# Layer 0's z rows and gates in two DRAM tensors, each gathered on its own

## The reference, cut to what matters

```
probs = softmax(z @ Wr + br)              # 8 experts
gate  = probs * keep                      # the most likely experts up to a mass of 0.8
h = relu(einsum('bth,ehf->betf', z, W1) + b1)      # F = 1024
y = einsum('betf,efh->beth', h, W2) + b2
out = einsum('bte,beth->bth', gate, y)
```

## Time and profile before

| | before |
|---|---|
| median of 3 runs | 1335.82 us (1334.29 to 1337.52) |
| the profiled execution: its own time | 1337.58 us |
| its span in the profile | 1335.9 us, so 1.7 us lie around the span |
| PE busy / DVE / ACT / POOL | 85% / 74% / 49% / 37% |
| layer 0's block loop | from about 188 us to about 650 us of the span |
| gathers of layer 0 on POOL | 76, mean 2.77 us |
| gathers of layers 1 and 2 on POOL (rows of 1,024 bytes) | 44, mean 1.19 us |

### The profile page before, as it was taken

One profiled execution on the slowest core, in us unless ns is written; L12 is line 12 of the kernel. 1 busy time (PEld: TensorE's weight loads), 2 busy tenths in 40 slices (PEclk: granted clock), 3 DMA queues, 4 the chain that ended last, 5 costly groups with the idle time before them and its releaser, 6 DMA issues.

```text
span 1335.9 us, 26939 instructions
## 1 busy us (share of the span) xinstructions
PE 1138.6 (85%) x8142; PEld 1057.5 (79%) x8142; DVE 989.0 (74%) x1721; ACT 651.8 (49%) x1361; POOL 500.0 (37%) x341
## 2 busy tenths in 40 slices
PE   5788959999999999999477489978479686899997
PEld 3677848999999999999446389977379665788886
DVE  6656967888888888888576587756468648777775
ACT  3433336667776677766044276622157352122222
POOL 5000026888888788786200234420057400000000
PEclk8899969999999999999778689998589887999999
DMA  7400435777777767775501276523078500000001
GB/s 188 148 23 2 174 127 165 232 236 216 238 242 241 237 217 231 236 244 147 147 6 64 82 265 244 200 81 104 24 230 263 171 30 1 24 25 24 24 24 63
DMA packets 77172, 188.28 MB, mean 141 GB/s; under 512 B 14147, under 2 KB 52291, under 8 KB 64835
## 3 DMA queue, kind: packets, MB, share of 16 engines
q1 hardware_dynamic: 55394, 148.06, 32.5%
q0 software_dynamic: 21728, 39.65, 12.2%
HBM read 157.18 MB, written 30.49 MB: 140 GB/s over the span
## 4 chain that ended last, share of the span: by engine, by line
PE 68%; DVE 15%; issue 8%; DMA 5%; ACT 2%; POOL 1%; DVEq 1%; SPq 0%; POOLq 0%; ACTq 0%
PE ps L678 22%; PE ps L679 21%; PE ps L680 21%; PE ps L802 2%; DVE hidden_lo L1416 2%; DMA scratch<-in_L_w 1%; DVE x_tok L1786 1%; DVE featA_lo L1416 1%; PE ps L690 1%; DMA y_rows<-w_raw,slot_rows 1%; DVE x_tok L1742 1%; DMA b_block<-in_L_ffn_b 1%; DVE w_lo L1416 1%; DVE hidden_f L1775 1%; DMA z_tok<-y_rows 1%
## 5 line engine op out<-in xcount | busy, mean ns | idle before, releaser
L1215 ACT ACTIVATE hidden_f<-ps,b_block 128x256 f32<-128x256 f32 x432 | 221.4, 513 | 177.9 <-PE ps L680 168.5
L582 POOL DMA_INDIRECT x_tok<-z_gate_rows,slot_rows x76 | 210.6, 2771 | 231.3 <-DVE slot_rows L1570 155.8
L1416 DVE TENSOR_TENSOR hidden_lo<-hidden_f,hidden_hi 128x512 fp32r<-128x512 f32 x300 | 195.3, 692 | 68.2 <-ACT hidden_hi L1252 36.6
L1216 ACT ACTIVATE hidden_hi<-ps,b_block 128x256 fp32r<-128x256 f32 x432 | 223.2, 517 | 0.0
L678 PE MATMUL ps<-w_hi,featA_hi 128*128 128x256 f32 (+1 forms) x624 | 178.7, 286 | 7.4 <-DVE w_lo L1416 3.4
L679 PE MATMUL ps<-w_lo,featA_hi 128*128 128x256 f32 (+1 forms) x624 | 177.7, 285 | 0.0
L680 PE MATMUL ps<-w_hi,featA_lo 128*128 128x256 f32 (+1 forms) x624 | 177.7, 285 | 0.0
L678 PE MATMUL ps<-featB_hi,hidden_hi 128*128 128x256 f32 x608 | 173.3, 285 | 0.0
L679 PE MATMUL ps<-featB_lo,hidden_hi 128*128 128x256 f32 x608 | 171.4, 282 | 0.0
L680 PE MATMUL ps<-featB_hi,hidden_lo 128*128 128x256 f32 x608 | 170.3, 280 | 0.0
L608 POOL DMA_INDIRECT x_rows<-w_raw,slot_rows x76 | 124.6, 1639 | 37.2 <-issue 21.9
(11 more groups left out here) (386 smaller groups left out, 3143.8 us busy)
## 6 DMA issues: line engine op xcount, KB each, us to landing
scratch<-in_L_w SPq DMA_DIRECT2D x48, 1024.0 KB
z_tok<-in_L_w SPq DMA_DIRECT2D x29, 1024.0 KB
x_tok<-in_L_w SPq DMA_DIRECT2D x19, 1024.0 KB
b_block<-in_L_ffn_b POOLq DMA_DIRECT2D x60, 128.0 KB, 3.6
z_tok<-in_L_w SPq DMA_DIRECT2D x12, 512.0 KB
scratch<-in_L_w SPq DMA_DIRECT2D x12, 512.0 KB
z_rows<-z_tok SPq DMA_DIRECT2D x8, 512.0 KB, 2.9
z_tok<-y_rows SPq DMA_DIRECT2D x8, 512.0 KB, 5.5
```

The lines of the kernel that those rows point to most:

```text
L582: gp.indirect_dma_start(XBL[L][:, k, tt, :], None, ZD if L else ZD0, bass.IndirectOffsetOnAxis(ap=TOK[:, q * BTT + tt:q * BTT + tt + 1], a ...
L1215: act.activation(HF[:, f // 2, part], ps, func, bias=b1)
L1216: act.activation(HTh[:, k, f // 2, part], ps, func, bias=b1).then_inc(s_hhi[L], 1)
L1416: return nc.vector.tensor_tensor(out, full, hi.bitcast(F32), ALU.subtract)
```

## The change

`ZD0` is now 256 floats wide, rows of 1,024 bytes. The gates go to a DRAM tensor of their own, `GD0`, with rows of 8 floats (32 bytes). Behind each gather of z rows POOL issues a second one with the same index column, for the gates, into a new view `XG0` of the same tile. Both add to the same semaphore, so the waits of PE and DVE ask for 64 for each block of layer 0 in place of 32 (`XBN`). The number of SP's stores is as before. Lines behind the change are up to six further down: POOL's gather of z is L584 and that of gates L588.

```
-ZW0 = D + 8
-        ZD0 = nc.dram_tensor("z0_gate_rows", [ROWS, ZW0], F32).ap()
+        ZD0 = nc.dram_tensor("z0_rows", [ROWS, D], F32).ap()
+        GD0 = nc.dram_tensor("gate_rows", [ROWS, 8], F32).ap()
-        XB0 = X[:].rearrange("p t d -> p (t d)")[:, 0:2 * BTT * ZW0].rearrange("p (b t d) -> p b t d", b=2, t=BTT)
+        XB0 = X[:].rearrange("p t d -> p (t d)")[:, 0:2 * BTT * D].rearrange("p (b t d) -> p b t d", b=2, t=BTT)
+        XG0 = X[:].rearrange("p t d -> p (t d)")[:, 2 * BTT * D:2 * BTT * (D + 8)].rearrange("p (b t e) -> p b t e", b=2, t=BTT)
+        XBN = [16 * BTT * n for n in (2, 1, 1)]
-                for rows, src in ((ZD0[:, 0:D], X[:, 0:DUMPS, :]), (ZD0[:, D:ZW0], X[:, 0:DUMPS, 0:8]),
+                for rows, src in ((ZD0, X[:, 0:DUMPS, :]), (GD0, X[:, 0:DUMPS, 0:8]),
-                sp.dma_start(ZD0[0:B * SEQ].rearrange("(t p) d -> p t d", p=P)[:, :, D:ZW0], G[:, :, 0:8]).then_inc(s_zd, 16)
+                sp.dma_start(GD0[0:B * SEQ].rearrange("(t p) d -> p t d", p=P), G[:, :, 0:8]).then_inc(s_zd, 16)
...
                     gp.indirect_dma_start(XBL[L][:, k, tt, :], None, ZD if L else ZD0,
                                           bass.IndirectOffsetOnAxis(ap=TOK[:, q * BTT + tt:q * BTT + tt + 1], axis=0)
                                           ).then_inc(s_xb[L][k], 16)
+                    if L == 0:
+                        gp.indirect_dma_start(XG0[:, k, tt, :], None, GD0,
+                                              bass.IndirectOffsetOnAxis(ap=TOK[:, q * BTT + tt:q * BTT + tt + 1], axis=0)
+                                              ).then_inc(s_xb[0][k], 16)
...
-                    pe.wait_ge(s_xb[L][k], i * (16 * BTT) + 16 * BTT)
+                    pe.wait_ge(s_xb[L][k], i * XBN[L] + XBN[L])
...
-                    dve.wait_ge(s_xb[0][k], i * (16 * BTT) + 16 * BTT)
+                    dve.wait_ge(s_xb[0][k], i * XBN[0] + XBN[0])
-                    nc.vector.tensor_scalar(GBK[:, k, :], XB0[:, k, :, bass.ds(e + D, 1)].rearrange("p t o -> p (t o)"),
+                    nc.vector.tensor_scalar(GBK[:, k, :], XG0[:, k, :, bass.ds(e, 1)].rearrange("p t o -> p (t o)"),
```

More of the change, by code:

```diff
@@ L397, in z_rows @@
                     sp.wait_ge(s_zd, 16 * (5 + c))
-                    sp.dma_start(ZD0[0:B * SEQ].rearrange("(t p) d -> p t d", p=P)[:, c * TPC:(c + 1) * TPC, 0:D],
+                    sp.dma_start(ZD0[0:B * SEQ].rearrange("(t p) d -> p t d", p=P)[:, c * TPC:(c + 1) * TPC, :],
                                  Z[:, c * TPC:(c + 1) * TPC, :]).then_inc(s_zd, 16)
```

## The result

| | before | after |
|---|---|---|
| median of 4 runs | 1335.24 us (1334.29 to 1337.52) | 1380.94 us (1380.06 to 1385.04) |
| ratio, 95% interval | | 1.0346 (1.0321 to 1.037) |
| profiled execution | 1337.6 us | 1381.06 us |
| its span | 1335.9 us | 1379.4 us |

The changed kernel is 3.5% slower. The direction was predicted, the size was not: 1344 was forecast, and 1380.94 lies above the range.

What follows compares the result with a forecast made beforehand. PE was taken to bound the steady loop, with POOL's work free until PE waits. Terms 4.4 + 3.1 + 0.4 = +7.9 us on the profiled 1337.6 gave 1345.5, or 1344 for the median; range 1339.5 to 1361.

Steps and rivals of the forecast that it cites:

- What a gather costs: On POOL: 0.95 us whatever the row's size, entering only between DVE's two-read SBUF instructions and not ending inside a CAST.
- First block (T1): Loop's start: PE's first transposes wait for four gathers instead of two, with a 4.55 us landing: +4.4 us.
- Third block (T2): Loop's start: PE waits for step 1's four gathers, transposing at 212.7 instead of 208.45 us; net +3.1 us.
- the stop that is gone: Third block: PE's 1.22 us wait for ACT, behind DVE's bias add and the bias rows, was to cost nothing new.
- this clock: Ahead of the third block's transposes: PE idles 4.3 us and may fall to 1.2 GHz, adding up to 3 us.
- Loop (T3): Steady block loop: added gathers fit POOL's spare time, 17 steps cost 0, with +0.4 us left once at the end.
- the half step closes: Steady loop: POOL, free at 623.2 us, is ready for the next gathers in time, so PE keeps its pace.
- DMA engines: Each step's 512 added 32-byte rows cost 0, as nothing in the loop waits for a transfer.
- the loop bound by POOL: Rival: gathers missing DVE's subtract boundaries add 0.6 to 1.8 us a step, 1354 to 1375 us; chance 0.30.

Runs made afterwards that it cites:

- e3: Kernel after with its second gather widened from 32 to 1,024 bytes a row, taking the z row again (wrong gate numbers): 1398.63 us, ratio 1.0471.
- e4: Kernel after with DVE's large W1 subtract, large CAST and large W2 subtract in layer 0 cut into four pieces each: 1347.66 us, ratio 1.0088.
- e9: Kernel after with only DVE's large W1 subtract in layer 0 cut into two halves: 1355.52 us, ratio 1.0091.
- e11: Kernel after with layer 0's W1 subtract in halves and the first two blocks' bias rows issued ahead of step 1's gathers: 1358.77 us, ratio 1.0135.
- e6: Kernel after with DVE's two large subtracts of layer 0 in four pieces each and its large CAST whole: 1344.89 us, ratio 1.0052.
- e5: Kernel before plus one added 32-byte gather for each layer 0 block (38, not 76), which only POOL waits for: 1343.14 us, ratio 1.0046.
- e2: Kernel after without its gate gathers, the gate column read from the 1,024-byte z row (wrong gate numbers): 1350.0 us, ratio 1.0097.
- e12: Kernel before with only the subtracts ahead of the loop in four pieces and the first two blocks' bias rows ahead of the next gathers: 1336.24 us, ratio 0.9967.
- e7: Kernel before with DVE's two large subtracts and large CAST of layer 0 in four pieces each: 1338.62 us, ratio 1.0015.

## Why the prediction was wrong, by its own steps

**What a gather costs** was right: 0.95 us of its own, independent of the row's size, and the rest is waiting for DVE. The 152 gathers took 218.4 us where 76 had taken 210.6; e3 shows by experiment that the row's size is not in it, and e4 that DVE's long instructions are.

**First block (T1), +4.4:** right. The entry's rows after the change, POOL and PE:

```profile
180.63 1.10 POOL L584 DMA_INDIRECT x_tok<-z_rows,slot_rows  x1 [157.21 <-DVE slot_rows L1576]
182.04 2.56 POOL L588 DMA_INDIRECT x_tok<-gate_rows,slot_rows  x1 [0.30 <-issue]
...
187.08 1.89 POOL L588 DMA_INDIRECT x_tok<-gate_rows,slot_rows  x1 [0.30 <-issue]
...
208.42 0.94 POOL L584 DMA_INDIRECT x_tok<-z_rows,slot_rows  x1 [14.45 <-DVE block_gates L1694]
...
215.66 0.94 POOL L588 DMA_INDIRECT x_tok<-gate_rows,slot_rows  x1 [0.30 <-issue]
```

```profile
193.94 1.11 PE L808 MATMUL ps<-ident,x_tok 128*128 128x128 f32 x4 [15.07 <-DMA x_tok<-gate_rows,slot_rows]
```

```profile
220.39 1.11 PE L808 MATMUL ps<-ident,x_tok 128*128 128x128 f32 x4 [5.70 <-DMA x_tok<-gate_rows,slot_rows]
```

From the first gather to the transposes it is 13.31 us, and it was 8.50: +4.8. The four gathers took exactly the slots forecast, 8.34 us (180.63 to 188.97), and the landing 4.97 us where 4.55 was taken.

**Third block (T2), +3.1:** the mechanism was half right and the size too small, +6.8 (12.8, less 1.2 and 4.8). The four gathers ended 8.18 us after the first began, where 8.58 was forecast. The landing took 3.79 us (216.60 to 220.39) and not 1.96. After that wait of 5.70 us PE works at its lower level: the transposes of 1.11 us are twice the 0.60 us of the second block's. The windows show the clock, from the third block's transposes to the fourth's, first after the change and then before:

```profile
220.39:226.00 5.61, 5.61 (x28) 5.61 (x29) 0.69 (x1) 2.62 (x3) 2.14 (x3) 0.53 0.73 194
226.00:234.66 8.66, 8.66 (x76) 8.66 (x75) 5.30 (x8) 4.68 (x14) 2.73 (x2) 1.00 0.01 2
```

```profile
208.45:221.86 13.41, 12.19 (x101) 11.98 (x102) 7.37 (x13) 6.82 (x15) 5.04 (x5) 1.00 0.62 197
```

The stretch takes 14.27 us without a stop, and it took 13.41 us with the stop of 1.22 us. PE needed 2.1 us more for it than its 12.19 us before. So the 6.8 us add up: 5.7 from the first gather of step 1 to the transposes (11.97 us in place of 6.25; 4.3 forecast), 0.2 because that gather comes later behind the first transposes, less 1.2 for the stop that is gone, as forecast, and 2.1 of clock. The prediction kept this clock as an unknown of up to 3 us outside its sum, and there it belonged inside. The bias rows, on which the step's stop was hung, make no difference to this stretch (e9 and e11).

**Loop (T3), +0.4:** this is the step that failed; the loop cost 29.8 us. "two scatters of 1.6 + 0.3 behind 619.05 [...] free at 623.2" gives the second scatter its floor. By the prediction's own numbers it would start at about 620.95, beside the gate column at 620.63 (later by 0.4), with the large subtract right behind. No row of before showed a scatter that starts there, so the price should have been bounded by what DVE then runs: a large subtract and a CAST, 3.5 us. The trace after has 3.58 us at 485.75. With 2 us more in place of 0, "the half step closes" is false: POOL starts its next gathers late, the next scatters later, and in the trace only a stall brings them back. That chain was tested: the same instructions stall nowhere once DVE's long subtracts are cut (e4, e6), nor in e11, where the gathers are still held and the scatters are not, and half of the added gathers fit ahead of the threshold (e5). The sum had a second gap: it has no term for PE's clock in the loop, which fell behind each stall and makes up about 11 of the 29.8 us.

**DMA engines, 0:** right in the loop within 2 us for the bytes (e2, e3).

**The rival that came closest** was the loop bound by POOL, at 0.30. It had the right engine and even a threshold of some 0.6 us, but priced its worst case at 1.8 us a step, 1375. It looked only at gathers that miss a gap, and not at the two scatters. The lock that the prediction read in the rows was thus applied to one kind of POOL's instructions and not to the other. The Trainium skill (SBUF — State Buffer, Who interferes with whom) calls the shared port pair an exclusive lock. The scatters of 3.58 us under a subtract and a CAST agree with a lock. The page's sentence that tensor_tensor did not stall a DMA disagrees with them, as with the gather of 2.54 us that takes 0.96 us in e12, where the subtract beside it is in pieces.

**What stays open:** why the bias rows took 7.9 us to land behind two held scatters; and which of e12's two edits brings its gain. A version that releases the output buffer ahead of the gathers wasn't tried.

## What to carry to other kernels

When instructions are added to an engine that is "free" beside a saturated one, walk its whole cycle and ask of every later instruction, not only of the added ones, what it now starts beside. An instruction that slides from 1.06 us before a long neighbour to 0.15 us behind its start costs 2 us more, and in this trace that lateness grew until a stall reset it. A busy share cannot show this: POOL was at 80% before and 83% after. Where such a hold is suspected, cutting the holder into pieces is the test, and cutting it only where the path is short of time may bring a small gain (e12, 0.3%).

## What the runs showed of the hardware that was not expected

- An accumulating scatter is held by DVE's large instructions as a gather is: 1.6 us free, 3.58 us beside one subtract and one CAST.
- With DVE's subtract in four pieces the gathers beside it at the entry take 0.96 us, as when DVE leaves POOL alone, and 1.12 to 1.18 us on average in all of layer 0 (e4). The pieces cost DVE about 0.2 us for each large instruction (2.50 us against 2.29), and the loop got 8 to 9 us longer with them (e4, e7).
- A lag that grows in steps shows as a period: five stalls of 4.6 to 6.4 us, one in six blocks, and half steps of mostly 11.85 us between them.
- A wait on PE can cost more than its length: behind the one of 3.24 us that ended at 525.71 the granted clock was 0.54 for 3.75 us, and behind the one of 5.70 us that ended at 220.39 it was 0.53 for 5.61 us.
